# The second mixture of experts: down products with tokens on the partitions, its gate weights applied there, and three of its four blocks moved among the causal attention batches

## What is computed

```python
    def _moe(x, gate, w1, w2, w3):
        xf = x.reshape(-1, D)
        probs = jax.nn.softmax(xf @ gate, axis=-1)
        w, idx = jax.lax.top_k(probs, TOP_K)          # TOP_K = 2 of 4
        w = w / jnp.sum(w, axis=-1, keepdims=True)
        oh = jax.nn.one_hot(idx, N_EXPERTS, dtype=xf.dtype)
        comb = jnp.einsum('nk,nke->ne', w, oh)
        out = jnp.zeros_like(xf)
        for e in range(N_EXPERTS):
            h = jax.nn.silu(xf @ w1[e]) * (xf @ w3[e])
            out = out + comb[:, e:e + 1] * (h @ w2[e])
    ...
    x = x + _attention(_rmsnorm(x, g1), wq, wk, wv, wo)
    x = x + _moe(_rmsnorm(x, g2), gate, w1, w2, w3)
```

## Time and profile before

| | |
|---|---|
| median of 3 runs | 1395.15 us (1392.28 to 1397.72) |
| the profiled execution | 1398.62 us, of which the span of the trace 1396.8 us |
| mean granted TensorE clock | 0.896 of full speed |
| busy: PE, DVE, ACT, POOL | 1163.5, 795.7, 641.3, 362.3 us |
| causal batches 27 to 31 | about 1100 to 1226 us |
| second mixture behind them | about 1226 to 1397 us |

### The profile page before, as it was taken

The page is one execution under the profiler, slowest core; times in us unless marked ns, Lnnn a source line. Parts: engine busy times, 40 slices in busy tenths (PEclk is TensorE's granted clock), DMA queues, the critical chain, the costliest instruction groups (busy, mean ns, idle before and its releaser), DMA issues. The chain is left out here.

```text
span 1396.8 us, 24402 instructions
## 1 busy us (share of the span) xinstructions
PE 1163.5 (83%) x8324; PEld 659.1 (47%) x8324; DVE 795.7 (57%) x1863; ACT 641.3 (46%) x1047; POOL 362.3 (26%) x958
## 2 busy tenths in 40 slices
PE   2798988898886687888888988888978877879998
PEld 1244444576443574444444444434555655534343
DVE  2577777434765114676777668586566655433433
ACT  1366654554653333655466545444433433423333
POOL 2332213421335113434322213221143332100000
PEclk9999988899887788888899998988989888879999
DMA  8444334463335342565454534423252433121010
GB/s 231 144 137 132 108 108 141 147 178 90 106 96 158 116 137 66 170 177 166 151 153 133 149 95 126 126 83 93 85 155 76 147 104 104 38 57 46 1 30 15
DMA packets 173810, 159.75 MB, mean 114 GB/s; under 512 B 12745, under 2 KB 147273, under 8 KB 173641
## 3 DMA queue, kind: packets, MB, share of 16 engines
q1 hardware_dynamic: 169496, 143.07, 34.6%
q0 software_dynamic: 4192, 15.12, 3.5%
HBM read 92.61 MB, written 67.63 MB: 115 GB/s over the span
## 5 line engine op out<-in xcount | busy, mean ns | idle before, releaser
L1052 ACT ACTIVATE prob<-e_ps 128x1024 f32<-128x1024 f32 (+1 forms) x384 | 375.2, 989 | 230.5 <-PE e_ps L1574 154.2
L1219 DVE TENSOR_REDUCE nmax<-s_ps 128x1 f32<-128x512 f32 x512 | 332.3, 684 | 173.7 <-PE s_ps L1537 171.7
L1574 PE MATMUL e_ps<-Qst,Kst 75*128 75x256 bf16 x1408 | 252.8, 295 | 10.6 <-ACT prob L1052 4.1
L1537 PE MATMUL s_ps<-Kst,Qst 72*128 72x512 bf16 x512 | 206.4, 420 | 59.0 <-DVE nmax L1219 51.2
L1590 PE MATMUL av_ps<-prob,Vx 128*32 128x256 f32 (+1 forms) x3072 | 231.0, 425 | 0.0
L1574 PEld LDWEIGHTS e_ps<-Qst,Kst 75*128 75x128 bf16 x1408 | 135.6, 104 | 123.4 <-issue 72.1
L1590 PEld LDWEIGHTS av_ps<-prob,Vx 128*32 128x32 f32 x3072 | 87.3, 119 | 92.7 <-issue 62.2
L976 POOL TENSOR_TENSOR mparts<-nmax,zeros 128x8 bf16<-128x8 f32 x128 | 26.9, 210 | 392.5 <-issue 381.9
L1055 ACT ACTIVATE OT<-av_ps 128x256 f32<-128x256 f32 x128 | 49.3, 385 | 170.4 <-PE av_ps L1590 169.7
L1228 DVE TENSOR_REDUCE nmax<-s_ps 128x2 f32<-128x512 f32 x128 | 85.7, 686 | 63.0 <-PE s_ps L1551 62.5
L1537 PEld LDWEIGHTS s_ps<-Kst,Qst 72*128 72x128 bf16 x512 | 52.6, 103 | 120.2 <-DVE nmax L1219 83.0
(11 more groups left out here) (202 smaller groups left out, 1775.1 us busy)
## 6 DMA issues: line engine op xcount, KB each, us to landing
q_parts<-qp SPq DMA_DIRECT2D x96, 192.0 KB, 2.4
k_parts<-kp SPq DMA_DIRECT2D x48, 384.0 KB, 3.3
Qst<-q_parts SPq DMA_DIRECT2D x128, 144.0 KB
Kst<-k_parts SPq DMA_DIRECT2D x64, 288.0 KB
k_parts<-kp SPq DMA_DIRECT2D x48, 192.0 KB, 2.6
Kst<-k_parts SPq DMA_DIRECT2D x64, 144.0 KB
ctxT<-in_ctxT SPq DMA_DIRECT2D x16, 256.0 KB, 4.6
FB<-xs_rows SPq DMA_DIRECT2D x22, 128.0 KB, 2.2
```

What stands on the lines that cost most here:

```text
L1052: act.activation(dst, src, ACT.Exp).then_inc(e_drained, 1)
L1219: ve.tensor_reduce(nmax[:, g, u, h % GH:h % GH + 1], s_ps[:, c % 2, :], AX.X, ALU.max, negate=True).then_inc(s_drained, 1)
L1537: last = pe.matmul(s_ps[:, c % 2, :], Qst[0:ROWS, par, s, u * P:u * P + P], Ks[0:ROWS, par, s, :], start=True, stop=True)
L1574: last = pe.matmul(o, Ks[0:KROWS, par, h, t * P:t * P + P], Qst[0:KROWS, par, h, :], start=True, stop=not a.rope)
```

## The change

m1.down is now one step for an expert: for each 128 tokens three matmuls with the tokens as the stationary side, so that tokens come out on the partitions, into `misc`. VectorE adds it to the residual with `comb` as its scalar for each token. Spread, mask, the masked features, m1.y and m1.back are gone, and both matmuls of m1.h read the same features. Silu is made from Tanh, which leaves the buffer of `e_ps` full until VectorE has done two instructions on it (`m1.mul`): (tanh(a/2) + 1) a, and that times b; the missing half is in `comb`. Blocks 0 and 1 stand in batches 27 to 28 and 29 to 30 from slot 3 of the first, one tile a slot, and the first five tiles of block 2 in batch 31; `moe1_steps` keeps the other seven and block 3. The whole input of a block is loaded where its features for the gate were (`m1.load` in place of `m1.gload`); block 3's behind the last batch's nT.

```diff
+def expert_steps(i, k):
+    steps = []
+    if k:
+        steps.append(("m1.mul", i, ((k - 1) // T1, (k - 1) % T1)))
+    if k < E1 * T1:
+        steps.append(("m1.h", i, (k // T1, k % T1)))
+    return steps
+def expert_down(i, k):
+    return [("m1.down", i, k // T1 - 1)] if k and k % T1 == 0 else []
+def moe1_items():
+    for i in range(NBLK - 1):
+        for k in range(E1 * T1 + 1):
+            at = (2 * i + 3) * slots + 3 + k
+            steps = expert_steps(i, k)
+            if at < B * slots:
+                it[(3 * B + at // slots, at % slots)] = steps + expert_down(i, k)
...
+            else:
+                left.append((i, k))
@@ body
-        units[1:1] = [[st] for st in tiles if st[0] == "m0.h"]
+        units[1:1] = [[st] for st in tiles if st[0] in ("m0.h", "m1.h")]
...
         out.append(("E", n, s))
+        out += [st for st in tiles if st[0] == "m1.mul"]
@@ moe1_steps
+    extra = {k: [st] for k, st in zip((0, 1, 2, 4, 6, 7), post)}
+    extra[7].append(("m1.load", i, None))
+    work = MOE1_LEFT + [(i, k) for k in range(E1 * T1 + 1)]
+    first = len(MOE1_LEFT)
+    extra.setdefault(first, []).append(("m1.gate", i, None))
+    for k in range(5):
+        extra.setdefault(first + k // 2, []).append(("m1.choose", i, k))
+    for x, (blk, k) in enumerate(work):
+        out += expert_steps(blk, k) + expert_down(blk, k) + extra.get(x, [])
@@ ScalarE
-                    act.activation(prob[:, RING_AT[st] % RING, 0:BLK], e_ps[:, c % 2, 0:BLK], ACT.Silu)
-                    act.activation(prob[:, RING_AT[st] % RING, BLK:2 * BLK], e_ps[:, c % 2, BLK:2 * BLK], ACT.Copy) \
+                    act.activation(prob[:, RING_AT[st] % RING, 0:BLK], e_ps[:, c % 2, 0:BLK], ACT.Tanh, scale=0.5) \
                         .then_inc(e_drained, 1)
@@ VectorE
+                elif kind == "m1.mul":
+                    hid = prob[:, RING_AT[h] % RING, 0:BLK]
+                    ve.wait_ge(e_drained, c + 1)
+                    ve.scalar_tensor_tensor(out=hid, in0=hid, scalar=1.0, in1=e_ps[:, c % 2, 0:BLK], op0=ALU.add,
+                                            op1=ALU.mult)
+                    ve.drain()
+                    ve.tensor_tensor(hid, e_ps[:, c % 2, BLK:2 * BLK], hid, ALU.mult).then_inc(m1_gated, 1)
+                elif kind == "m1.down":
+                    acc = m1_res[par]
                     ve.wait_ge(misc_filled, MISC[st] + 1)
...
+                    for t in range(BT):
+                        last = ve.scalar_tensor_tensor(out=acc[:, t, :], in0=misc[:, t * D:t * D + D],
+                                                       scalar=comb[:, n, t, arg:arg + 1], in1=acc[:, t, :], op0=ALU.mult,
+                                                       op1=ALU.add)
+                    last.then_inc(misc_drained, 1)
+                    if arg == E1 - 1:
+                        ve.drain()
+                        ve.scalar_tensor_tensor(out=m1_res2[par], in0=acc, scalar=gate_of("moe1"), in1=m1_res2[par],
+                                                op0=ALU.mult, op1=ALU.add).then_inc(m1_made, 1)
@@ TensorE
+            def slot_free(c):
+                pe.wait_ge(e_drained, c - 1)
+                kind, n, arg = SLOT_STEP[c - 2]
+                if kind == "m1.h":
+                    pe.wait_ge(m1_gated, M1MUL[("m1.mul", n, arg)] + 1)
...
                 elif kind == "m1.down":
...
+                    pe.wait_ge(m1_gated, M1MUL[("m1.mul", n, (arg, T1 - 1))] + 1)
+                    for x in range(BT):
+                        for t in range(T1):
+                            tokens = prob[:, RING_AT[("m1.h", n, (arg, t))] % RING, x * P:x * P + P]
+                            last = pe.matmul(misc[:, x * D:x * D + D], tokens, w2_1[:, arg, t, :], start=t == 0,
+                                             stop=t == T1 - 1)
+                    last.then_inc(misc_filled, 1)
```

More of the change, by code:

```diff
@@ L89 @@
 MISC_KINDS = ("xT", "q", "k", "v", "maxT", "ctx", "aT", "proj", "nT", "f.back", "f.nT", "m0.gate", "m0.rank",
-              "m0.xT", "m0.down", "m1.gate", "m1.spread", "m1.mask", "m1.back")
+              "m0.xT", "m0.down", "m1.gate", "m1.down")
 E_KINDS = ("E", "m0.h", "f.h", "m1.h")
@@ L323, in body @@
             units += [[("AV", n - 1, (NG - 1, x))] for x in range(p.avs) if (x + 1) * a.gs // p.avs - 1 == s]
-        tiles = TILE_ITEMS.get((n, s), [])
-        units[1:1] = [[st] for st in tiles if st[0] == "m0.h"]
+        tiles = TILE_ITEMS.get((n, s), []) + MOE1_ITEMS.get((n, s), [])
+        units[1:1] = [[st] for st in tiles if st[0] in ("m0.h", "m1.h")]
         chunks = [[]]
         for p in range(per * s, per * s + per):
-            for st in items[p] + [st for st in tiles if st[0] != "m0.h" and p % per == per - 1]:
+            for st in items[p] + [st for st in tiles
+                                   if st[0] in ("m0.xT", "m0.down", "m1.down", "m1.store") and p % per == per - 1]:
                 if st[0] in MISC_KINDS:
@@ L443 @@
 UNIT = count(("S",))
[L444 to L445 removed]
+GROUP = count(("AV", "f.down"), lambda st: st[0] != "AV" or st[2][1] == att(st[1]).avs - 1)
+M1MUL = count(("m1.mul",))
+SLOT_STEP = {c: st for st, c in SLOT.items()}
 def slot(n, s):
@@ L470, in ring_users @@
         else:
-            user[c] = ("m1", M1H[st] + 1)
+            user[c] = ("misc", MISC[("m1.down", st[1], st[2][0])] + 1)
     return user
@@ L1039, in prob_free @@
                     which, need = USER[RING_AT[st] - RING]
-                    act.wait_ge(av_filled if which == "av" else m1_used, need)
+                    act.wait_ge(av_filled if which == "av" else misc_filled, need)
             def step(kind, n, arg):
@@ L1709, in moe1_step @@
                 if kind == "m1.gate":
-                    pe.wait_ge(m1_gin[par], 16 * (n // 2 + 1))
+                    pe.wait_ge(m1_loaded[par], 48 * (n // 2 + 1))
                     for t in range(BT):
-                        last = pe.matmul(misc[:, t * E1:t * E1 + E1], m1_g[par][:, t * P:t * P + P], gw1[:, :],
+                        last = pe.matmul(misc[:, t * E1:t * E1 + E1], m1_x[par][:, t * P:t * P + P], gw1[:, :],
                                          start=True, stop=True)
                     last.then_inc(misc_filled, 1)
-                elif kind == "m1.spread":
-                    pe.wait_ge(m1_chosen, n + 1)
-                    for t in range(BT):
-                        last = pe.transpose(misc[0:E1, t * P:t * P + P], comb[:, n, t, :], ident[:, :])
-                    last.then_inc(misc_filled, 1)
-                elif kind == "m1.mask":
-                    sel = ident[0:E1, arg:arg + 1].to_broadcast([E1, P])
-                    pe.matmul(misc[:, :], sel, ohTf[0:E1, :], start=True, stop=True).then_inc(misc_filled, 1)
                 elif kind == "m1.h":
```

142 lines of the change are left out of this document (27 added, 115 removed).

## The result

| | before | after |
|---|---|---|
| median of 4 runs each, us | 1396.43 (1392.28 to 1408.83) | 1430.49 (1420.40 to 1438.93) |
| the profiled execution, us | 1398.62 | 1436.96 |
| span of its trace, us | 1396.8 | 1433.8 |

The changed kernel takes 1.0187 of the time before (95% interval 1.0131 to 1.0243). It is slower, and its median lies above 1412, the upper end of the range that was given.

The account below looks back on a forecast made before the run. TensorE, busy for 83% of the span, was taken as the bound, with holes in the batches. Tail -77, batches +72 and clock +3 gave -2 on 1398.6: 1396.6 us (1393 for a median), range 1372 to 1412.

Parts of the forecast that it names:

- The two large terms: The tail shrinks from 171 to 94 us, -77; batches 27 to 31 grow by +72 with the work moved in.
- +3 for the clock: Batches: waits of 3.9 us can drop TensorE's clock, 1 us each in three batches.
- the part on the batches: Batches 27 to 31: slot-by-slot count of moved tiles, down products and waits, +72 together.
- 10 of other work: Batches 27 and 29, AV of slot 3 to slot 7: TensorE's work besides the moved tiles and down product, 10 us.
- near 10: Batch 28: new waits of tiles, down products and nT turn, with 0.6 for misc, near 10 us, making it 47.
- Rival C: Batches: frequent waits bring 1.2 GHz for a third of each batch, +15, 1408 us; sign: clock below about 0.85; chance 0.28.
- The pitch: Tail: 9.7 us an expert between down products, for 7.73 of TensorE work.
- Step 1: Tail: block 2's tiles 5 to 11, three down products, batch 31's last AV, turns and projection, and waits: 33 us.
- What goes away on TensorE: Tail: masks, spreads, turns and the last block's own end removed, some 22 us in all.
- The two operations without a row: VectorE: scalar_tensor_tensor from PSUM on 512 columns, taken 0.75 us; gate-weighted addition, four taken as 1.2 us.
- Rivals B and D: Batches and tail: B, VectorE keeps ahead, 1378 us, chance 0.27; D, tiles fill holes almost wholly, 1365 us, chance 0.07.
- A: Whole kernel: the main forecast, within 0.5% (7 us) of the time before, 1386 to 1400 us, chance 0.38.

Follow-up runs that it names:

- free_early: Changed kernel, but ScalarE copies both halves of a tile out of e_ps, so the buffer is free before VectorE's multiply; 1414.20 us, 1.0084 of the kernel before.
- no_choice_after: Changed kernel without the softmax and the selection of two experts, raw logits as gate weights; one run, 1423.27 us.
- all_tail: Changed kernel's new arithmetic without the move, all four blocks in the tail; 1400.23 us, 1.0035 of the kernel before.
- early_post: Changed kernel with the last batch's output steps at tail positions 0 to 5, so block 3's load is issued earlier; 1416.56 us, 1.0132 of the kernel before.

## Why the prediction was wrong

**The sum as forecast and as measured.** The two large terms were -77 and +72, with +3 for the clock: -2. Their border in the changed kernel was the end of block 2's fifth tile. That tile lies behind the last nT mark, so the tables above have it in the tail:

```profile
1333.92 1.87 PE L1712 MATMUL e_ps<-FB,wbig 128*128 128x512 f32 x2
...
1337.43 0.86 PE L1582 MATMUL av_ps<-prob,Vx 128*32 128x256 f32 x16
```

With the border at 1337.43, measured are +106.9 for the batches and -74.5 for the tail, together +32.4. The miss of 34.4 is 34.9 in the batches and 2.5 in the tail, less the 3 that were given for the clock. (The base of the 171 us, "the nT turn of batch 30 (1225.8)", is that of batch 31.)

By batch, the sum's marks were the AVs of slot 7. In the tables' marks, which stand ahead of these AVs, one tile (1.7) of batches 27, 29 and 31 and the last down product (2.6) of batches 28 and 30 belong to the next stretch. So read, the forecast was +7.2, +22.7, +8.1, +24.8 and +7.6 for batches 27 to 31, 70.4 together. Measured are +14.1, +28.2, +19.1, +27.0 and +15.2, 103.6.

**The step that failed** is in the part on the batches. For 27, 29 and 31 the walk priced "10 of other work, four tiles and a down product 9.5, 1.6 for the down product that waits for its last multiply, 3.9 for nT behind choice, addition and multiply", and no wait of a tile for its buffer. It gives no reason; for batches 28 and 30 it has such waits. Tiles and E units take turns at the two buffers, so in every slot a tile comes back to the buffer of the tile just before it, and needs its multiply. That wait is 4.3, 4.3 and 3.7 us in 27, 29 and 31, 12.3 together, hardly less than in batches 28 and 30 (4.9, 4.8); the loads, 1.5, 1.3 and 1.7, come on top, with 1 of it in the sum. Against this the nT wait was 2.8 and not 3.9. The forecast thus had TensorE idle for 10.6 us less than before in these three batches (its differences less the tiles and down products); the tables have 10.0 more. That is 20.6 of the miss. free_early shows that the buffer is the cause of most: with the wait taken away all five batches are 19.5 us shorter. no_choice_after shows that the choice in front of the multiply makes 3.4 of the 12.3 and not the whole: my first account of these waits, formed from the row with 3.28 us, was wrong.

**The base of all batches was too low.** The walk took TensorE's other work in batch 28 as 17.5, "23.4 less the 4.3 of nT, 0.6 of the slow AV and about 1 of smaller waits". The table of stretches gives 20.25 busy in batch 28 and 18.58 in batch 30. The "10 of other work" from the AV of slot 3 to that of slot 7 is 10.89, 12.40 and 11.27 busy in batches 27, 29 and 31. The 4.3 was the gap between two rows of the chain, and a chain leaves out what an engine does beside it. The timeline of TensorE in the kernel before, at the same place:

```profile
1145.18 0.22 PE L1547 MATMUL s_ps<-maskb,identb 128*128 128x128 bf16 x1
1147.43 0.41 PE L1523 MATMUL misc<-ident,normed 128*128 128x128 f32 x2 [2.04 <-DVE normed L1319]
```

S units ran until 1145.4, and the idle time was 2.04. So the reading that a wait of more than 4 us put TensorE at 1.2 GHz there was wrong too: it was about 2. There were 3.5 us of idle time to be filled in batch 28 and 2.8 in batch 30, where I had counted nearly 6. The waits put in their place, "near 10", were a little high, 8.6 and 9.2, so in these two batches the idle time was missed by only 1.9 together.

**The clock was mis-sized.** Forecast +3 for the batches, measured 9.1 as busy time above the full-speed price (1.9, 3.8, 3.2, 1.2 and -1.0 by batch). Rival C had it as the slower case, but set its mark at a granted clock under 0.85. The clock of the batches is 0.93, higher than the 0.87 before. A mean over a stretch was the wrong test: the tiles are what runs at 1.2 GHz, since they stand right behind the waits. C's sign was right; its cause, the clock, accounts for 9 of the 33 by which batches 27 to 31 came out longer, and idle time for 22.5.

**The tail was right in kind.** The last block's load wait was 9, measured 8.83. The stretch from there to the end of its first down product was 18, measured 18.2 (1379.64 to 1397.87). The pitch was 9.7, measured 9.89. The end, three experts with gate and store, was 34, measured 35.9 (1397.87 to 1433.8): the last down product starts in step but takes 4.24 in place of 2.92, behind a wait of 2.27.

```profile
1424.78 4.24 PE L1720 MATMUL misc<-wbig,prob 128*128 128x128 f32 x24 [2.27 <-DVE prob L1469]
```

Step 1, 33, took 33.4 (1337.43 to 1370.8). What goes away on TensorE was priced at 22 us; all_tail has 17.3 less busy time in its tail, which holds one gate more than before. The two operations without a row were priced well: the multiply's first half 0.68 (taken 0.75), four additions 1.13 (taken 1.2).

**Rivals B and D**, VectorE ahead or holes filled, counted on less waiting than A; there was more. What the batches could have given at best is their 27.1 us of idle time (and what their matmuls at 1.2 GHz lose), and filling them with tiles that wait for VectorE brought 21.6 more.

## What to carry to other kernels

Before work is moved into a stretch to fill it, take the stretch's idle time from its busy time, not from the gaps in the chain; it is the most that the move can bring, and each moved piece brings its own waits. For each moved instruction ask which buffer of a ring it comes back to and which engine frees it, in the order in which others take turns at the ring. Where an engine's queue has a short step that waits for a long product, let the independent step go ahead of it: a down product came 1.3 us sooner after the one before wherever nothing else stood in that queue (9.88 to 8.62). With this order and the choice spread out the tail of the version without the move fell from 182.7 to 159.4, while the move, with its faults mended, only met the kernel before.

## What the runs showed beside this

- A wait cost more than its length. Taking 9.3 us of idle time from the batches (free_early) took 10.2 us of busy time too, from the same matmuls. In the tail 8.5 less idle time went with 4.3 less busy time (early_post), where single traces differ by 2.2.
- The same instructions up to batch 26 ended anywhere within 16 us (1085.76 to 1101.64) in twelve traces. In the batches of the three versions with the same instructions there, idle time repeated within 0.5 us and busy time only within 6.0.
- A scalar_tensor_tensor on 512 columns takes 0.68 us with one source in PSUM and 0.69 with both in SBUF (free_early's multiply), less than the 0.75 of the earlier trace rows, which has both in SBUF too; what makes that one longer is open. On 128 columns, with a scalar for each partition, four in a row take 1.13.
